# Fetching two chunks of eight instead of three on TensorE in a graph network's message passes

## The reference, cut to what matters

```python
# weighted (twice, with W_self, W_neigh of l = 0, 1)
msg = h[src] * edge_weight[:, None]
h_neigh = segment_sum(msg, dst, n) * inv_deg
h = h @ W_self[l].T + h_neigh @ W_neigh[l].T + b_neigh[l]
# attribute (twice, with a0, W0 and a1, W1)
a0 = a_mu0 + exp(a_ls0) * edge_attr_64
h = h * norm_out
agg = segment_sum(h[src] * a0, dst, n)
h = agg * norm_in @ W0 + b0
```

## Time and profile before

| | us |
|---|---|
| median of 3 runs | 10290.76 |
| lowest and highest run | 10283.23, 10292.5 |
| the profiled execution: its own time | 10281.51 |
| its span | 10279.7 |
| TensorE busy (matmuls) | 7855.9 (76%) |
| VectorE busy | 7916.7 (77%) |
| ScalarE busy | 2340.4 (23%) |
| GpSimd busy | 5302.1 (52%) |
| mean granted TensorE clock | 0.803 |

### The profile page before, as it was taken

One profiled execution on the slowest core, in us unless ns is written; L12 is line 12 of the kernel. 1 busy time (PEld: TensorE's weight loads), 2 busy tenths in 40 slices (PEclk: granted clock), 3 DMA queues, 4 the chain that ended last, 5 costly groups with the idle time before them and its releaser, 6 DMA issues. The chain is left out here.

```text
span 10279.7 us, 176764 instructions
## 1 busy us (share of the span) xinstructions
PE 7855.9 (76%) x44549; PEld 5592.7 (54%) x44550; DVE 7916.7 (77%) x11192; ACT 2340.4 (23%) x8740; POOL 5302.1 (52%) x5215
## 2 busy tenths in 40 slices
PE   6999999899999975665458566553776776777768
PEld 5777777677767753333257433332773443744437
DVE  8888666688888867777789777778997666876668
ACT  2222455200000011111179311111880000000000
POOL 4554555455455527777500277772005776057760
PEclk9999999899999977777755677776557666976669
DMA  3333444455455537777569577773993333333334
GB/s 96 103 102 97 131 137 137 111 138 137 121 138 138 137 86 252 250 250 249 177 258 411 204 250 250 249 248 99 389 378 100 98 97 83 113 110 97 98 75 116
DMA packets 829924, 1724.39 MB, mean 168 GB/s; under 512 B 378906, under 2 KB 462711, under 8 KB 774297
## 3 DMA queue, kind: packets, MB, share of 16 engines
q1 hardware_dynamic: 456542, 1159.65, 32.5%
q0 software_dynamic: 193584, 397.91, 15.3%
q10 hardware_dynamic: 179712, 165.79, 4.9%
HBM read 1277.89 MB, written 444.85 MB: 168 GB/s over the span
## 5 line engine op out<-in xcount | busy, mean ns | idle before, releaser
L697 PE MATMUL ps_G<-table_parts,low_onehots 125*128 125x320 bf16 x21840 | 3471.5, 321 | 113.3 <-DVE rows_by_feature L727 57.0
L697 PEld LDWEIGHTS ps_G<-table_parts,low_onehots 125*128 125x128 bf16 x21840 | 2221.2, 104 | 1194.6 <-DVE rows_by_feature L727 151.8
L532 POOL DMA_INDIRECT gathered_rows<-node_table,index x2080 | 1982.0, 953 | 1655.6 <-PE ps_sum L552 938.0
L532 POOL DMA_INDIRECT gathered_rows<-xl_table,index x1664 | 1925.7, 1157 | 1423.7 <-PEq L1505 917.3
L1517 PE MATMUL ps_Z<-xr,onehots_wide 125*128 x3328 | 1462.6, 607 | 994.1 <-DVE z L1565 973.3
L532 POOL DMA_INDIRECT gathered_rows<-rel_table,index x1456 | 1384.7, 951 | 1552.4 <-ACT index L522 1109.3
L552 PE MATMUL ps_sum<-messages,onehots 128*125 128x65 f32 (+3 forms) x13312 | 1925.1, 309 | 227.6 <-DVE messages L1914 183.0
L552 PEld LDWEIGHTS ps_sum<-messages,onehots 128*125 128x125 f32 x13312 | 1858.4, 224 | 295.3 <-issue 283.4
L1517 PEld LDWEIGHTS ps_Z<-xr,onehots_wide 125*128 125x128 f32 x3328 | 836.1, 263 | 1620.6 <-issue 1514.5
L727 DVE TENSOR_TENSOR rows_by_feature<-ps_G,fifth_onehots 128x320 f32<-128x320 f32 x1456 | 707.2, 486 | 639.6 <-PE ps_G L697 635.2
L1565 DVE TENSOR_TENSOR z<-gathered_rows,ps_Z 128x650 f32<-128x650 f32 x832 | 652.4, 825 | 645.1 <-DMA gathered_rows<-xl_table,index 645.1
(11 more groups left out here) (329 smaller groups left out, 6575.0 us busy)
## 6 DMA issues: line engine op xcount, KB each, us to landing
stash_a<-gathered_rows SPq DMA_DIRECT2D x208, 1300.0 KB
kept_rows<-stash_a SPq DMA_DIRECT2D x208, 1300.0 KB
onehots<-onehots_kept SPq DMA_DIRECT2D x520, 500.0 KB
onehots_turned<-onehots_turned SPq DMA_DIRECT2D x416, 256.0 KB
low_rows<-low_rows SPq DMA_DIRECT2D x416, 192.0 KB
stash_r<-gathered_rows ACTq DMA_DIRECT2D x208, 272.0 KB
kept_rows<-stash_r SPq DMA_DIRECT2D x208, 272.0 KB
onehots_kept<-onehots ACTq DMA_DIRECT2D x104, 500.0 KB
```

Source lines behind the costliest of these rows:

```text
L532: pool.indirect_dma_start(G[:, HALF * k + q, 0:width], None, table, bass.IndirectOffsetOnAxis(IDX[:, k, q:q + 1], 0)).then_inc(gathered[k] ...
L697: last = nc.tensor.matmul(ps_G[:, (fetch * k + g) % 2, 0:D * FIVE], OT[0:BN, k, g, a, :], HP[:, part, a, :, :].rearrange("p f b -> p (f b) ...
```

## The change

One constant changes. It sets, in both weighted and both attribute passes, how many chunks of a group TensorE fetches, and by HALF - FETCH how many GpSimd gathers.

```diff
@@ -36,7 +36,7 @@
 PAIR = 2 * HALF
 NG = NS // HALF
 PER = 7
-FETCH = 3
+FETCH = 2
 FIVE = 5
 BANK = 512
 R = 8
```

## The result

The changed kernel takes **9945.64 us** (median of 4, 9942.75 to 9950.33); the kernel before took 10291.4 beside it. The ratio is 0.9666, 95% interval 0.9649 to 0.9683: 3.3% faster. The forecast was 9947 us.

A forecast was written before the change was run, and what follows sets the result against it. TensorE was taken to bound the four passes before, GpSimd after, at 7.49 us per group. Savings of 106.3, 83.7, 76.9 and 77 us sum to 344; 10290.76 - 344 = 9947 us, range 9915 to 10020.

The forecast's parts named there:

- The bound: Weighted and attribute passes: GpSimd's six gathers at 1.249 us, 7.49 us per group, exceed TensorE's 6.30 and VectorE's 5.6.
- The passes: First three of the four passes end at 884.0, 1814.2, 2734.5 us; the four save 106.3, 83.7, 76.9 and 77 us.
- The tail: End of each pass: 7.9 us from the last gather's start to the last messages, bounds 1 and 8.6 us.
- The sum: Savings of the four passes total 344 us, taken from the median 10290.76 us to give 9947 us.
- TensorE's part: Per group in the four passes: 15 of 45 fetch matmuls go, 2.12 us, so 8.42 us becomes 6.30.
- The 6.2 us for ScalarE and TensorE in turn: Second weighted pass, per group: ScalarE's own 4.3 us, 6.2 us even with TensorE's 1.94 us of sums between.
- TensorE stays the bound: Rival for the four passes: all 883 us gained, 9408 us, needing gathers 1.05 us apart; chance 0.01.
- the signs: Things expected in the profile after, among them passes of 780 to 800 us and about a microsecond's TensorE wait per group.
- The clock rival: Rival for the four passes: gaps put TensorE's sums at half clock, losing some 218 us of gain, 10165 us; chance 0.08.
- The small instruction: Rival: VectorE's 0.17 us fifth onehots delay one gather per group in the four passes, 71 us, 10018 us; chance 0.05.
- The gather queue: Rival: six gathers per group in the four passes slow to 1.46 us each, 175 us slower, 10466 us; chance 0.03.

## Why the prediction was right

**The bound.** That GpSimd becomes the bound, at 6 x 1.249 = 7.49 us, was the step that carried everything, and it is shown from both sides: with seven gathers the time rises by 1.24 us a group, with five it falls by 1.27 in the attribute passes. It was read from starts 40 gathers apart in an untouched stage, not from the 0.94 us of one gather. Six times 0.94 would have been 5.6 us, and TensorE would have looked like the bound.

**The passes.** Ends forecast, in the coordinates of before: 884.0, 1814.2, 2734.5. Measured: 883.74, 1707.58 + 106.6 = 1814.1, 2544.28 + 190.3 = 2734.6. The savings are 106.6, 83.8, 76.8 and 76.9 us against 106.3, 83.7, 76.9 and 77. That the second pass saves less because its gathers begin late held too. That the ends agree to a few tenths is partly luck: in the first pass the last gather started 0.6 us earlier than forecast (869.00 for 869.6) and its tail was 0.6 us longer (8.5 for 7.9), and the end of the first attribute pass came 5.1 us after its last messages, where I had 4.4.

**The tail.** I took 7.9 us from the last gather to the messages; it is 8.5, 8.0 and 7.6 in three passes. The size was right, by analogy with the earlier trace rows, but the reason given (the end of a stage) was incomplete: 4.9 of the 8.5 us go away when the padding edges name different rows.

**The sum.** 344.0 us came from the passes, and 5.2 us were given back behind them, where the change does nothing; the other kernels with the padding as it was lie between 6571.5 and 6577.4 for the same stages where the kernel before takes 10284. So the spans differ by 338.8 us, the medians by 345.8. That the median came out 1 us from the forecast is luck: it makes up the 5.2 us because the profiled execution of the kernel before lay 10 us under its median and that of the changed one only 3.

**TensorE's part** was the weakest term. 8.42 - 2.12 = 6.30 us is its work; as a bound it would be 6.78 and 7.22 in the weighted passes, by the run with five gathers. The 6.2 us for ScalarE and TensorE in turn in the second weighted pass was too low in the same way: that pass is the one of 7.22. It did no harm because 7.49 lies above both. The rival "TensorE stays the bound", priced at 9408 us, should have been some 0.5 to 0.9 us a group dearer in these passes. Three of the signs came otherwise than stated. TensorE does not wait a microsecond for messages in each group: in the first pass it waits 30 times for 104 groups, 1.6 us on the mean and up to 7.2. The passes were to last 780 to 800 us and last 771, 798, 769 and 771; the forecast's own end of the first pass, 884.0, already meant 771. And the stages behind became 5.2 us longer.

**The clock rival** was right in its premise and wrong in its effect. The granted clock did fall, to 0.93 to 0.96, with TensorE at half speed for microseconds after a gap, and to 0.67 with seven gathers. In neither does the pace follow it: the gathers keep 1.249 us. The reason given against the rival, a slowed TensorE fills its own gap, is what the timeline from 300 to 322 us shows.

**The small instruction** that would hold the gathers up does not. At 300.91 the fifth onehots, two inputs in SBUF, begin 0.04 us before a gather, and that gather takes 0.95 us. In the four passes 65 gathers start while such an instruction runs, and none of them takes more than 0.95 us. In a whole pass of 624 gathers three intervals are over 1.4 us, all at its start, beside the instructions that make the table parts (L670 to L674, among them the long subtraction of the earlier trace rows); in the first pass they cost 4.5 us together. The rule of the Trainium skill (SBUF — State Buffer, Who interferes with whom) agrees with those three and not with the 416 small ones; had it held there too, the kernel would be 71 us slower.

**The gather queue** did not slow down: the mean gather took 952 ns (953 before) at a DMA share of up to 0.58, and the same at 0.66 with five gathers.

## What to carry to other kernels

Take the rate of an engine that issues DMAs from the distance between starts where it waits for nothing, never from its busy share: here 74% busy was 100% occupied. When work is moved between two engines, write both engines' time per group as a line over the split and look for the crossing, allowing uneven splits within a turn; the bound from subtraction alone is too low by the waits in between (6.30 became 6.8 to 7.2). And look at what the padding of an index list points to.

## What the runs showed of the hardware

- Gathers whose 128 indices all name one table row land late: 8.5 us from the start of the last gather of the first pass to its reader, 3.7 with the indices spread; in all 52.6 us of this kernel.
- An indirect gather of 128 rows of 256 bytes costs 1.249 us of GpSimd's time (median distance of starts), whether five, six or seven are issued per group, beside TensorE at clock 0.67 or 0.99.
- The same kernel took 10284 and 10285 us on chip 1 and 11411 and 11419 on chips 8 and 3, and in the traces from there TensorE paused before instructions that wait for nothing (192 pauses with 119 us in 700 us of one of them). A gain of 1.9% by the sums (190 us) was none there. A forecast from one trace holds for the conditions of that trace.
